# State space stage: three of the six exponentials of a batch stay in PSUM, and VectorE's work stands in another order

## The chip, the cores and the metric

One core of a Trainium2 chip runs the whole program. The metric is device time in microseconds, the median of the runs. Five engines run side by side, each in its own order, and meet only at semaphores: TensorE (PE, and PEld for its weight loads), VectorE (DVE), ScalarE (ACT), GpSimd (POOL), and the queue of SyncE (SP) that issues most DMAs.

## The reference, cut to what matters

The program is a decoder of two layers. The change is in the state space block, the first sublayer of the second layer, for 16 batches of 256 rows:

```
dt = softplus(dt + dt_bias);  A = -exp(A_log)
decay = exp(A * dt_t)
state = state * decay + (x_t * dt_t) * B_t        # for every t, 8 heads of 64, 128 states
y_t = einsum('bhpn,bn->bhp', state, C_t)
y = y + x_part * D_full
y = y * silu(z)
y = y * rsqrt(mean(y * y) + EPS) * norm_w
out = y @ out_proj_w.T
```

## The kernel before

`state_space` doesn't scan. It treats the 256 rows of a batch as two blocks of 128 and writes the scan as a product with a 128x128 matrix per head and block pair: exp(sum of A dt between the two rows) times the product of C and B. There are three block pairs (first with first, first with second, second with second) and 8 heads, so six tiles of 128x512 (four heads each), numbered u = 0 to 5; u // 2 is the block pair and u % 2 the half of the heads. For each u:

- `exponents(n, u)`, TensorE: two matmuls of 128x512 put the exponents of batch n into PSUM bank `e_ps[u % 2]`. So u = 0, 2, 4 share `e_ps[0]` and u = 1, 3, 5 share `e_ps[1]`. Before it writes u, it waits until the bank's last exponential was read (`decay_ready`).
- `decays(n, u)`, ScalarE: one exponential, from the bank into `mat[:, u]` in SBUF.
- `matrices(eng, n, u, ready)`: one multiplication of `mat[:, u]` by `gm`, the masked product of B and C, in place. VectorE does u = 0, 2, 4 (`low_mat_ready`), GpSimd u = 1, 3, 5 (`high_mat_ready`).
- `mix(n, blk)`, TensorE: multiplies the three finished tiles of one half of the heads by the scaled rows `xdt`.

Around them lie: `masked_products` (VectorE, makes `gm` from bank `g_ps`), `taps` (VectorE, three passes of the convolution over one projection bank `in_ps`, which frees that bank for the next `project`), `sum_experts` (VectorE, the input of batch n + 5: adds the experts' rows and takes their moments; then `scale_x` on GpSimd makes the norm's factors and ScalarE's `normalize_x` applies them), `tail_rows`, `high_terms` (VectorE, `rhs_hi` of the next batch's exponents; GpSimd's `low_terms` makes `rhs_lo`), `mean_squares`, `skip_terms`, `residual`, `gated`, `row_moments`, and `scaled_rows`, which makes `xdt` of the next batch from rows that `to_rows` has transposed into the two `e_ps` banks. `gather` on GpSimd issues the four indirect DMAs of batch n + 7.

The order on each engine is written out by hand in a loop over n (`STEPS`), with one branch for even and one for odd n, since the projections are done once for a pair of batches. In these loops two places matter for the argument. On ScalarE, in an even step, `decays(n, 1)` and `decays(n, 2)` stand behind `normalize_x(n + 4)`:

```
                    first_tap(n, 1)
                    if real(n + 4):
                        normalize_x(n + 4)
                    if now:
                        decays(n, 1)
                        decays(n, 2)
```

On GpSimd, in an odd step, `scale_x(n + 5)`, for which that `normalize_x` waits, stands behind `low_terms`, `scale_y` and `gather`, and the next even step begins with `split_y`'s products just done and u = 1 and 3 of `matrices`. `state_products(n)` on TensorE opens a batch; `project(n, i)` are six matmuls each, between the exponents.

## Time and profile before

| | us |
|---|---|
| median of 3 runs | 2675.45 (2670.41 to 2675.78) |
| the profiled execution | 2671.63 |
| its span | 2669.9 |
| the 16 batches of the state space stage | 1650 to 2030 of the span |

Outside that stretch the change touches no instruction that works on data. In the page the stage lies in slices 25 to 30 of 40. A busy engine there isn't yet a bound: the views further down show, in order of time, who waits for whom. In a timeline row the number in brackets is the idle time of the engine just before, and the arrow names what ended it; a row without brackets followed on the one ahead of it.

### The profile page before, as it was taken

What the parts mean: (1) busy time and instruction counts of PE and PEld (TensorE: products, weight loads), DVE (VectorE), ACT (ScalarE), POOL (GpSimd) and SP (SyncE); (2) the same over time, 40 slices, a digit from 0 to 9 for tenths busy, and PEclk for the clock granted to TensorE, in tenths of its full rate; (3) what the DMA queues carried; (4) which work ended last, traced back from release to release, by engine and by line L of the source; (5) the groups of instructions that cost most, each with busy time, mean ns of one, the idle gap of its engine ahead of it and who ended that gap; (6) DMA issues with size and microseconds to landing.
All of it is one profiled execution on the core that took longest, in us unless ns stands there. A gap on an engine that the chain in (4) does not pass through costs nothing. (4 is left out here: it accounts for less than half of the span.)

```text
span 2669.9 us, 63255 instructions
## 1 busy us (share of the span) xinstructions
PE 2341.5 (88%) x23480; PEld 1968.6 (74%) x23480; DVE 1950.1 (73%) x3223; ACT 1423.5 (53%) x2223; POOL 1619.4 (61%) x1937
## 2 busy tenths in 40 slices
PE   5999999997799877998999965988995899987998
PEld 4677777775566656998999964777774666756998
DVE  2677777776589872646888857999984588875776
ACT  2566666664466652335666544655652466653333
POOL 3667666764467751275666656777764587863443
PEclk9899999999899987999999987998996799988999
DMA  8566666551889841146666652111002887841111
GB/s 205 131 159 159 160 145 158 153 120 43 245 216 229 219 111 36 52 138 204 224 228 226 230 175 64 41 48 32 21 13 85 213 225 208 224 105 41 53 54 52
DMA packets 227288, 363.44 MB, mean 136 GB/s; under 512 B 51968, under 2 KB 156416, under 8 KB 219520
## 3 DMA queue, kind: packets, MB, share of 16 engines
q1 hardware_dynamic: 207392, 281.32, 39.7%
q0 software_dynamic: 17376, 78.13, 8.6%
q8 instruction: 143, 2.34, 0.4%
q10 hardware_dynamic: 2304, 1.05, 0.2%
q14 instruction: 73, 0.60, 0.1%
HBM read 231.72 MB, written 133.69 MB: 137 GB/s over the span
## 5 line engine op out<-in xcount | busy, mean ns | idle before, releaser
L1369 ACT ACTIVATE self_probs<-self_score_ps 128x768 f32<-128x768 f32 x256 | 208.7, 815 | 183.9 <-PE self_score_ps L1271 182.0
L1585 POOL TENSOR_SCALAR_AFFINE_SELECT self_probs<-self_probs 128x512 f32<-128x512 f32 x256 | 169.5, 663 | 158.6 <-ACT self_probs L1369 158.6
L1506 DVE TENSOR_REDUCE self_neg_max<-self_max_ps 128x2 f32<-128x256 f32 x256 | 108.1, 422 | 165.1 <-PE self_max_ps L88 165.1
L647 ACT ACTIVATE cross_probs<-cross_score_ps 128x1024 f32<-128x1024 f32 x128 | 131.2, 1025 | 101.6 <-PE cross_score_ps L545 100.0
L745 DVE TENSOR_REDUCE cross_neg_max<-cross_max_ps 128x4 f32<-128x1024 f32 x128 | 154.9, 1212 | 39.1 <-PE cross_max_ps L524 39.0
L1507 DVE TENSOR_REDUCE self_neg_max<-self_max_ps 128x2 f32<-128x512 f32 x256 | 174.5, 682 | 0.0
L2297 POOL TENSOR_TENSOR moee_h_lo<-moee_h,moee_h_hi 128x512 fp32r<-128x512 f32 x78 | 112.5, 1442 | 92.3 <-ACT moee_h_hi L2034 91.6
L739 DVE TENSOR_REDUCE causal_block_max<-causal_max_ps 128x6 f32<-128x768 f32 x128 | 120.9, 946 | 56.4 <-PE causal_max_ps L88 55.9
L3592 POOL TENSOR_TENSOR ffn_g_lo<-ffn_g_full,ffn_g_hi 128x512 fp32r<-128x512 f32 x64 | 82.1, 1283 | 129.2 <-ACT ffn_g_hi L3478 116.9
L2034 ACT ACTIVATE moee_h_hi<-moee_h 128x512 fp32r<-128x512 f32 x110 | 69.6, 632 | 163.2 <-DVE moee_h L2200 163.2
L647 ACT ACTIVATE causal_probs<-causal_score_ps 128x768 f32<-128x768 f32 x128 | 103.6, 809 | 99.2 <-PE causal_score_ps L545 99.0
L79 PE MATMUL moee_g_ps<-moee_x_hi,moee_in_hi 128*128 128x256 f32 x440 | 131.3, 298 | 10.0 <-DVE moee_x_lo L2187 5.8
L1271 PE MATMUL self_score_ps<-self_q_stack,self_k_stack 49*128 49x128 f32 (+1 forms) x1024 | 129.0, 330 | 10.0 <-ACT self_probs L1369 6.4
L2200 DVE TENSOR_TENSOR moee_h<-moee_u_ps,moee_silu 128x512 f32<-128x512 f32 x110 | 75.5, 686 | 82.0 <-PE moee_u_ps L81 77.4
L2240 POOL DMA_INDIRECT x_tiles<-kept_x,moek_slot x64 | 65.8, 1029 | 107.1 <-issue 104.1
L79 PE MATMUL moee_y_ps<-moee_out_hi,moee_h_hi 128*128 128x256 f32 x440 | 125.4, 285 | 0.7 <-DVE moee_out_lo L2152 0.7
L81 PE MATMUL moee_g_ps<-moee_x_hi,moee_in_lo 128*128 128x256 f32 x440 | 125.7, 286 | 0.0
L79 PE MATMUL moee_u_ps<-moee_x_hi,moee_in_hi 128*128 128x256 f32 x440 | 125.7, 286 | 0.0
L80 PE MATMUL moee_g_ps<-moee_x_lo,moee_in_hi 128*128 128x256 f32 x440 | 125.7, 286 | 0.0
L80 PE MATMUL moee_u_ps<-moee_x_lo,moee_in_hi 128*128 128x256 f32 x440 | 125.1, 284 | 0.0
L81 PE MATMUL moee_u_ps<-moee_x_hi,moee_in_lo 128*128 128x256 f32 x440 | 125.1, 284 | 0.0
L81 PE MATMUL moee_y_ps<-moee_out_hi,moee_h_lo 128*128 128x256 f32 x440 | 124.9, 284 | 0.0
(507 smaller groups left out, 9479.9 us busy)
## 6 DMA issues: line engine op xcount, KB each, us to landing
self_q<-self_q_split SPq DMA_DIRECT2D x48, 512.0 KB, 3.5
self_q_raw<-self_q SPq DMA_DIRECT2D x32, 768.0 KB, 8.2
cross_stacks<-cross_qk SPq DMA_DIRECT2D x64, 384.0 KB, 6.4
causal_stacks<-causal_qk SPq DMA_DIRECT2D x64, 384.0 KB, 6.4
moe_y_tiles<-lasting_y_out SPq DMA_DIRECT2D x55, 256.0 KB, 2.5
mid<-lasting_y_out SPq DMA_DIRECT2D x48, 256.0 KB, 2.2
x_tiles<-zeros SPq DMA_DIRECT2D x16, 624.0 KB, 5.5
moee_xT<-x_tiles SPq DMA_DIRECT2D x39, 256.0 KB, 7.3
```

The costliest lines, as they stand in the source:

```text
L79: pe.matmul(out, a[0], b[0], start=start, stop=False, **kw)
L80: pe.matmul(out, a[0], b[1], start=False, stop=False, **kw)
L81: return pe.matmul(out, a[1], b[0], start=False, stop=stop, **kw)
L647: nc.scalar.activation(probs[i // 2][:, a, :, lo:], score_ps[:, :, lo:], ACT.Exp, scale=HD ** -0.5).then_inc(prob_ready, 1)
L739: last = dve.tensor_reduce(block_max[:, :, col % 4, :], bank[:, :, 0:3 * P].rearrange("p a (j t) -> p a j t", t=P), AX.X, ALU.max, negate= ...
L745: last = dve.tensor_reduce(neg_max[p][:, tile, :, col % 4, :], bank[:].rearrange("p a (q k) -> p a q k", q=QT), AX.X, ALU.max, negate=True)
L1271: last = pe.matmul(score_ps[:, ab, j * S + k * P:(j + 1) * S], k_stack[p][rows, tile, k * P:(k + 1) * P], q_stack[rows, 4 * tile + c, k * P:],
L1369: nc.scalar.activation(probs[g % 4][:, a, :, P:], score_ps[:, :, P:], ACT.Exp, scale=HD ** -0.5).then_inc(prob_ready, 1)
L1506: dve.tensor_reduce(neg_max[:, tile, :, c, 0:1], bank[:, :, 0:P], AX.X, ALU.max, negate=True)
L1507: dve.tensor_reduce(neg_max[:, tile, :, c, 1:2], bank[:, :, S:2 * S], AX.X, ALU.max, negate=True).then_inc(max_kept, 1)
L1585: pool.affine_select(diagonal, diagonal, [[0, 2], [0, 2], [1, P]], ALU.is_ge, zero, base=0, channel_multiplier=-1).then_inc(prob_masked, 1)
L2297: pool.tensor_tensor(h_lo[p][f][:].rearrange("p j s -> p (j s)"), h[f][:], h_hi[p][f][:].bitcast(F32).rearrange("p j s -> p (j s)"), ALU.s ...
```

## The change

Three things, all in the state space stage:

1. `decays(n, u)` for even u writes its exponential back into `e_ps[0]` in place of `mat`. `matrices` on VectorE reads it from there and writes `mat`; so one of its inputs lies in PSUM. Odd u is as before, on GpSimd.
2. The bank is now free only once VectorE has multiplied. `exponents(n, 2)` and `exponents(n, 4)` wait for `low_mat_ready` of u = 0 and u = 2, and `to_rows(n + 1)` of that bank waits for that of u = 4. The wait for `ssm_done` (that `mat` is free) moves from u = 0 on ScalarE to u = 1, and for u = 0 to VectorE.
3. VectorE's order is changed, so that the multiplications come sooner.

```diff
                 if u in (0, 2):
                     pe.wait_ge(rhi_ready, 2 * n + 1 + u // 2)
                     pe.wait_ge(rlo_ready, 2 * n + 1 + u // 2)
-                if u >= 2:
+                if u in (2, 4):
+                    pe.wait_ge(low_mat_ready, 3 * n + u // 2)
+                elif u >= 2:
                     pe.wait_ge(decay_ready, 6 * n + u - 1)
...
-                    if b:
-                        pe.wait_ge(decay_ready, 6 * b - 1 + q)
+                    if b and q == 0:
+                        pe.wait_ge(low_mat_ready, 3 * b)
+                    elif b:
+                        pe.wait_ge(decay_ready, 6 * b)
...
                 act.wait_ge(e_done, 6 * n + u + 1)
-                if u == 0 and n:
+                if u == 1 and n:
                     act.wait_ge(ssm_done, 2 * n)
-                nc.scalar.activation(mat[:, u, :, :].rearrange("p h t -> p (h t)"), e_ps[u % 2][:],
-                                     ACT.Exp).then_inc(decay_ready, 1)
+                dst = mat[:, u, :, :].rearrange("p h t -> p (h t)") if u % 2 else e_ps[0][:]
+                nc.scalar.activation(dst, e_ps[u % 2][:], ACT.Exp).then_inc(decay_ready, 1)
...
-            eng.tensor_tensor(mat[:, u, :, :], mat[:, u, :, :],
+            src = mat[:, u, :, :] if u % 2 else e_ps[0][:].rearrange("p (h t) -> p h t", t=P)
+            if u == 0 and n:
+                eng.wait_ge(ssm_done, 2 * n)
+            eng.tensor_tensor(mat[:, u, :, :], src,
```

VectorE, even batch (batch 4; the names are those of the section on the kernel). Before, `sum_experts` comes first (its last row here), then `gm`, `taps` 0 and 1 (three rows each), the multiplications of u = 0 and 2 together, `tail_rows`, `high_terms` and u = 4:

```order
L2859 BN_AGGR ssm_c_mv<-ssm_c_stats 128x2 x2
L2939 TENSOR_TENSOR ssm_gm<-ssm_g_ps,ssm_triang 128x384
L2893 SCALAR_TENSOR_TENSOR ssm_bc<-ssm_in_ps,ssm_cw,ssm_bc 128x2x255
L2893 SCALAR_TENSOR_TENSOR ssm_bc<-ssm_in_ps,ssm_cw,ssm_bc 128x2x254
L2893 SCALAR_TENSOR_TENSOR ssm_bc<-ssm_in_ps,ssm_cw,ssm_bc 128x2x253
L2893 SCALAR_TENSOR_TENSOR ssm_bc<-ssm_in_ps,ssm_cw,ssm_bc 128x2x255
L2893 SCALAR_TENSOR_TENSOR ssm_bc<-ssm_in_ps,ssm_cw,ssm_bc 128x2x254
L2893 SCALAR_TENSOR_TENSOR ssm_bc<-ssm_in_ps,ssm_cw,ssm_bc 128x2x253
L2827 TENSOR_TENSOR ssm_mat<-ssm_mat,ssm_gm 128x512 x2
L2947 TENSOR_TENSOR ssm_xdt_tail<-ssm_xdt,ssm_tail 128x512
L2930 TENSOR_TENSOR ssm_rhs_hi<-ssm_triang,ssm_a_hi 128x1024 x2
L2827 TENSOR_TENSOR ssm_mat<-ssm_mat,ssm_gm 128x512
```

Now the batch begins with `gm`; u = 0 stands ahead of `taps` 0, u = 2 between the two `taps`, and `sum_experts` behind them:

```order
L2946 TENSOR_TENSOR ssm_gm<-ssm_g_ps,ssm_triang 128x384
L2834 TENSOR_TENSOR ssm_mat<-ssm_e_ps,ssm_gm 128x512
L2900 SCALAR_TENSOR_TENSOR ssm_bc<-ssm_in_ps,ssm_cw,ssm_bc 128x2x255
L2900 SCALAR_TENSOR_TENSOR ssm_bc<-ssm_in_ps,ssm_cw,ssm_bc 128x2x254
L2900 SCALAR_TENSOR_TENSOR ssm_bc<-ssm_in_ps,ssm_cw,ssm_bc 128x2x253
L2834 TENSOR_TENSOR ssm_mat<-ssm_e_ps,ssm_gm 128x512
L2900 SCALAR_TENSOR_TENSOR ssm_bc<-ssm_in_ps,ssm_cw,ssm_bc 128x2x255
L2900 SCALAR_TENSOR_TENSOR ssm_bc<-ssm_in_ps,ssm_cw,ssm_bc 128x2x254
L2900 SCALAR_TENSOR_TENSOR ssm_bc<-ssm_in_ps,ssm_cw,ssm_bc 128x2x253
L2874 SCALAR_TENSOR_TENSOR ssm_y_shared<-ssm_y_routed,moek_weight,ssm_y_shared 128x256 x2
L2881 SCALAR_TENSOR_TENSOR ssm_x<-ssm_y_routed,moek_weight,ssm_y_shared 128x256 x2
L2862 BN_STATS ssm_c_stats<-ssm_x 128x6 x2
```

The same batch, some rows further on: `tail_rows`, then u = 4, which has moved ahead of `high_terms`, and `taps` 2:

```order
L2866 BN_AGGR ssm_c_mv<-ssm_c_stats 128x2 x2
L2954 TENSOR_TENSOR ssm_xdt_tail<-ssm_xdt,ssm_tail 128x512
L2834 TENSOR_TENSOR ssm_mat<-ssm_e_ps,ssm_gm 128x512
L2937 TENSOR_TENSOR ssm_rhs_hi<-ssm_triang,ssm_a_hi 128x1024 x2
L2900 SCALAR_TENSOR_TENSOR ssm_xs<-ssm_in_ps,ssm_cw,ssm_xs 128x2x255
L2900 SCALAR_TENSOR_TENSOR ssm_xs<-ssm_in_ps,ssm_cw,ssm_xs 128x2x254
L2900 SCALAR_TENSOR_TENSOR ssm_xs<-ssm_in_ps,ssm_cw,ssm_xs 128x2x253
```

What moved there: all three multiplications come earlier among VectorE's rows, and `sum_experts` and `high_terms` later.

VectorE, odd batch (batch 5). Before, u = 0 and 2 stand together behind `sum_experts`; u = 4 is the row after the last one here, behind `ms`:

```order
L2939 TENSOR_TENSOR ssm_gm<-ssm_g_ps,ssm_triang 128x384
L2867 SCALAR_TENSOR_TENSOR ssm_y_shared<-ssm_y_routed,moek_weight,ssm_y_shared 128x256 x2
L2874 SCALAR_TENSOR_TENSOR ssm_x<-ssm_y_routed,moek_weight,ssm_y_shared 128x256 x2
L2855 BN_STATS ssm_c_stats<-ssm_x 128x6 x2
L2857 MEMSET ssm_gate 128x1
L2859 BN_AGGR ssm_c_mv<-ssm_c_stats 128x2 x2
L2827 TENSOR_TENSOR ssm_mat<-ssm_mat,ssm_gm 128x512 x2
L2947 TENSOR_TENSOR ssm_xdt_tail<-ssm_xdt,ssm_tail 128x512
L2893 SCALAR_TENSOR_TENSOR ssm_xs<-ssm_in_ps,ssm_cw,ssm_xs 128x2x255
L2893 SCALAR_TENSOR_TENSOR ssm_xs<-ssm_in_ps,ssm_cw,ssm_xs 128x2x254
L2893 SCALAR_TENSOR_TENSOR ssm_xs<-ssm_in_ps,ssm_cw,ssm_xs 128x2x253
L2962 TENSOR_SCALAR ssm_ms<-ssm_g_ps 128x2
```

Now u = 0 stands ahead of `sum_experts` and u = 2 still behind it; u = 4 is the row after the last one here, ahead of `ms`:

```order
L2946 TENSOR_TENSOR ssm_gm<-ssm_g_ps,ssm_triang 128x384
L2834 TENSOR_TENSOR ssm_mat<-ssm_e_ps,ssm_gm 128x512
L2874 SCALAR_TENSOR_TENSOR ssm_y_shared<-ssm_y_routed,moek_weight,ssm_y_shared 128x256 x2
L2881 SCALAR_TENSOR_TENSOR ssm_x<-ssm_y_routed,moek_weight,ssm_y_shared 128x256 x2
L2862 BN_STATS ssm_c_stats<-ssm_x 128x6 x2
L2864 MEMSET ssm_gate 128x1
L2866 BN_AGGR ssm_c_mv<-ssm_c_stats 128x2 x2
L2834 TENSOR_TENSOR ssm_mat<-ssm_e_ps,ssm_gm 128x512
L2954 TENSOR_TENSOR ssm_xdt_tail<-ssm_xdt,ssm_tail 128x512
L2900 SCALAR_TENSOR_TENSOR ssm_xs<-ssm_in_ps,ssm_cw,ssm_xs 128x2x255
L2900 SCALAR_TENSOR_TENSOR ssm_xs<-ssm_in_ps,ssm_cw,ssm_xs 128x2x254
L2900 SCALAR_TENSOR_TENSOR ssm_xs<-ssm_in_ps,ssm_cw,ssm_xs 128x2x253
```

What moved there is u = 0, ahead of the eight rows or so of `sum_experts`, and `ms` behind u = 4. On the other engines no instruction that works on data moves.

## Rows read from the trace of the kernel before

**Rows 1.** Busy time by window: stretch, length, busy (instructions) by engine, clock, DMA.

```profile
1746.70:1796.70 50.00, 43.78 (x307) 37.09 (x307) 47.99 (x89) 30.24 (x50) 38.42 (x40) 0.97 0.15 43
```

**Rows 2.** Tiles ssm_mat and ssm_e_ps, instructions: min/median/max ns, first and last start.

```profile
L2827 DVE TENSOR_TENSOR ssm_mat<-ssm_mat,ssm_gm x48: 656/790/2387, 1658.3 to 2021.6; 128x512 f32<-128x512 f32 x48
...
L2955 DVE TENSOR_TENSOR ssm_xdt<-ssm_e_ps,ssm_dt x32: 656/681/691, 1646.1 to 2011.7; 128x512 f32<-128x512 f32 x32
```

**Rows 3.** Groups by line and shape, VectorE, 1650 to 2030 us.

```profile
L2827 DVE TENSOR_TENSOR ssm_mat<-ssm_mat,ssm_gm 128x512 f32<-128x512 f32 x48 | 52.3, 1110 | 6.4 <-ACT ssm_mat L2670 6.1
...
L2947 DVE TENSOR_TENSOR ssm_xdt_tail<-ssm_xdt,ssm_tail 128x512 f32<-128x512 f32 x16 | 18.5, 1157 | 0.0
```

**Rows 4.** Timeline, VectorE, batch 4: start, length, instruction [idle before <- releaser].

```profile
1743.74 3.01 DVE L2930 TENSOR_TENSOR ssm_rhs_hi<-ssm_triang,ssm_a_hi 128x1024 fp32r<-128x1024 f32 x2
1746.68 0.87 DVE L2867 SCALAR_TENSOR_TENSOR ssm_y_shared<-ssm_y_routed,moek_weight,ssm_y_shared 128x256 f32<-128x256 f32 x2
...
1749.45 0.52 DVE L2939 TENSOR_TENSOR ssm_gm<-ssm_g_ps,ssm_triang 128x384 f32<-128x384 f32 x1
1749.89 4.52 DVE L2893 SCALAR_TENSOR_TENSOR ssm_bc<-ssm_in_ps,ssm_cw,ssm_bc 128x510 f32<-128x510 f32 x6
1754.32 2.59 DVE L2827 TENSOR_TENSOR ssm_mat<-ssm_mat,ssm_gm 128x512 f32<-128x512 f32 x2
1756.84 1.77 DVE L2947 TENSOR_TENSOR ssm_xdt_tail<-ssm_xdt,ssm_tail 128x512 f32<-128x512 f32 x1
1758.53 2.35 DVE L2930 TENSOR_TENSOR ssm_rhs_hi<-ssm_triang,ssm_a_hi 128x1024 fp32r<-128x1024 f32 x2
1760.80 0.68 DVE L2827 TENSOR_TENSOR ssm_mat<-ssm_mat,ssm_gm 128x512 f32<-128x512 f32 x1
...
1766.34 0.87 DVE L2990 SCALAR_TENSOR_TENSOR ssm_yz<-ssm_xs,ssm_dcol,ssm_y_ps 128x256 f32<-128x256 f32 x2 [0.36 <-PE ssm_y_ps L2554]
...
1770.91 1.26 DVE L2955 TENSOR_TENSOR ssm_xdt<-ssm_e_ps,ssm_dt 128x512 f32<-128x512 f32 x2
```

**Rows 5.** Timeline, ScalarE, batch 4.

```profile
1748.71 0.60 ACT L2670 ACTIVATE ssm_mat<-ssm_e_ps 128x512 f32<-128x512 f32 x1
...
1752.25 1.09 ACT L2731 ACTIVATE ssm_x<-ssm_x,ssm_c_shift,ssm_c_rstd 128x256 f32<-128x256 f32 x2 [1.73 <-POOL ssm_c_shift L3102]
1753.25 1.06 ACT L2670 ACTIVATE ssm_mat<-ssm_e_ps 128x512 f32<-128x512 f32 x2
```

**Rows 6.** Timeline, GpSimd, batches 4 to 6.

```profile
1752.03 0.18 POOL L3102 TENSOR_TENSOR ssm_c_shift<-ssm_c_low,ssm_c_rstd 128x2 f32<-128x2 f32 x1
...
1771.14 0.23 POOL L3097 TENSOR_SCALAR ssm_var<-ssm_mv 128x2 f32<-128x2 f32 x1 [2.89 <-issue]
...
1788.46 1.90 POOL L3127 TENSOR_TENSOR ssm_rhs_lo<-ssm_triang,ssm_a_lo 128x1024 fp32r<-128x1024 f32 x1 [0.90 <-DVE ssm_a_lo L2924]
...
1802.04 0.18 POOL L3102 TENSOR_TENSOR ssm_c_shift<-ssm_c_low,ssm_c_rstd 128x2 f32<-128x2 f32 x1
```

**Rows 7.** Timeline, TensorE, batches 4 and 5.

```profile
1753.87 0.50 PE L2526 MATMUL ssm_e_ps<-ssm_rhs_hi,ssm_one_r 128*128 128x512 f32 x1 [3.72 <-ACT ssm_mat L2670]
...
1778.53 0.40 PE L2526 MATMUL ssm_e_ps<-ssm_rhs_hi,ssm_after 128*128 128x512 f32 x1
...
1785.87 0.40 PE L2552 MATMUL ssm_y_ps<-ssm_mat,ssm_xdt_tail 128*64 128x128 f32 x2 [1.63 <-DVE ssm_mat L2827]
```

**Rows 8.** Timeline, VectorE, batch 5, and the end of batch 6.

```profile
1775.46 1.91 DVE L2867 SCALAR_TENSOR_TENSOR ssm_y_shared<-ssm_y_routed,moek_weight,ssm_y_shared 128x256 f32<-128x256 f32 x2
...
1779.28 1.26 DVE L2827 TENSOR_TENSOR ssm_mat<-ssm_mat,ssm_gm 128x512 f32<-128x512 f32 x2
...
1783.35 2.37 DVE L2827 TENSOR_TENSOR ssm_mat<-ssm_mat,ssm_gm 128x512 f32<-128x512 f32 x1
1786.40 0.88 DVE L2971 SCALAR_TENSOR_TENSOR lasting_y_out<-ssm_xT_ps,ssm_row_scale,ssm_x 128x256 f32<-128x256 f32 x2 [0.68 <-issue]
...
1822.04 1.25 DVE L2955 TENSOR_TENSOR ssm_xdt<-ssm_e_ps,ssm_dt 128x512 f32<-128x512 f32 x2
```

More of the change, by code:

```diff
@@ L3010, in _ @@
                 if n % 2 == 0:
+                    if now:
+                        masked_products(n)
+                        matrices(dve, n, 0, low_mat_ready)
+                    taps(n, 0)
+                    if now:
+                        matrices(dve, n, 2, low_mat_ready)
+                    taps(n, 1)
                     if real(n + 5) and n != -2:
@@ L3013, in _ @@
                     if now:
-                        masked_products(n)
-                    taps(n, 0)
-                    taps(n, 1)
+                        tail_rows(n)
                     if now:
-                        matrices(dve, n, 0, low_mat_ready)
-                        matrices(dve, n, 2, low_mat_ready)
-                        tail_rows(n)
+                        matrices(dve, n, 4, low_mat_ready)
                     if n >= 0 and soon:
                         high_terms(n + 1)
-                    if now:
-                        matrices(dve, n, 4, low_mat_ready)
                     taps(n, 2)
@@ L3050, in _ @@
                         masked_products(n)
+                        matrices(dve, n, 0, low_mat_ready)
                     if real(n + 5):
@@ L3053, in _ @@
                     if now:
-                        matrices(dve, n, 0, low_mat_ready)
                         matrices(dve, n, 2, low_mat_ready)
@@ L3057, in _ @@
                     taps(n, 0)
+                    if now:
+                        matrices(dve, n, 4, low_mat_ready)
                     if late:
                         mean_squares(n - 1)
-                    if now:
-                        matrices(dve, n, 4, low_mat_ready)
                     if late:
```

## The prediction

> **What bounds the kernel now.** I read the windows first. In one period of two batches, 50.00 us long, VectorE is busy 47.99 us and TensorE 43.78 [rows 1]. So VectorE has 2 us of slack in 50, and the stage looks bound by it. The second look is at the length of its multiplications: at line L2827 they take from 656 to 2387 ns for one and the same shape [rows 2], 1110 ns in the mean, and `tail_rows` 1157 ns [rows 3]. A product that reads PSUM in one input (`scaled_rows`, same shape) takes 656 to 691 ns all 32 times [rows 2]. The long ones lie where GpSimd multiplies too. That is what the change goes for: 48 x (1110 - 680) = 20.6 us of stretching in `mat`, and 16 x (1157 - 680) = 7.6 us in `tail_rows`, beside it.
>
> The third look, at the timelines, is the one that decides. The even batch has a chain that doesn't run through VectorE's busy time. GpSimd ends `c_shift` of `scale_x` at 1752.03 [rows 6]; only then do ScalarE's `normalize_x` (1752.25, after 1.73 us of waiting) and, behind it, the exponentials of u = 1 and 2 run, which end at 1753.25 + 1.06 = 1754.31 [rows 5]. TensorE waits 3.72 us for them [rows 7]. VectorE doesn't wait: it spends this time on `sum_experts` and both `taps`, and comes to the multiplications at 1754.32, when u = 2 has just been done [rows 4]. So before, VectorE's order covers a late GpSimd exactly. I call R the end of `row_moments`, where `scaled_rows` starts (1770.91 for batch 4 [rows 4], 1822.04 for batch 6 [rows 8]). From R to the next `c_shift` are 1802.04 - 1770.91 = 31.13 us [rows 6]. There GpSimd goes through `scale_y` (1771.14), `scale_x`, `split_y`, `gather`, its products, the row scale, a short turn to VectorE for `residual` and `a_lo` (GpSimd idles 0.90 us for it at 1788.46), `low_terms` and the next `gather`. From `c_shift` to R are 1770.91 - 1752.03 = 18.88 us in batch 4 and 20.00 in batch 6. The sum of the two is the period.
>
> **The change, part by part.**
>
> *Multiplying from PSUM.* 48 instructions on VectorE lose their stretching. In a pair like 4 and 5: u = 0 and 2 of the even batch take 2.59 us for two [rows 4] where two unstretched ones take 1.26 [rows 8], so 1.33 less; `tail_rows` 1.77, or 0.68 once it no longer falls beside GpSimd's products, 1.09 less [rows 4]; u = 4 of the odd batch 2.37 [rows 8] against 0.68, 1.69 less. That is 4.1 us of VectorE's time in a pair. The ScalarE side is the same instruction with another target; no row shows a write back into its bank. I bound it by 0 to 0.6 us (the whole instruction, [rows 5]) for each of 48, and take 0, since it has idle time around it.
>
> The Trainium skill, "VectorE: DVE Perf Modes", section on the TRN2 errata, gives an instruction from PSUM 120 fixed cycles and one from SBUF 58; at its 0.96 GHz that would be an estimated 0.065 us more for each, 3.1 us for 48. The trace has the two alike, 681 ns and 680 or so for the unstretched ones, and the sum leaves it out.
>
> *VectorE's new order in the even batch.* After `rhs_hi`, at 1746.68 [rows 4], VectorE now needs `gm` at once. Before, `gm` came at 1749.45, with nothing to wait for; now it waits for TensorE's products of B and C, which I put at about 1747.4, 0.7 us. Then u = 0 needs the first exponential, 1748.71 + 0.60 = 1749.31 [rows 5]: 1.4 us more. It is followed by `taps` 0 (4.43 us for six rows [rows 4], so 2.22), to 1752.2; and u = 2 needs 1754.31: 2.1 us of waiting. Together 4.2 us of idle time, where there was none. What is queued behind it: `taps` 1, `sum_experts`, `tail_rows`, u = 4, `high_terms`, `taps` 2 and 3. From `c_shift` on the sum is: to the end of the second exponential 2.28 and to VectorE 0.05; u = 2 0.60; `taps` 1 2.22; `sum_experts` 1749.45 - 1746.68 = 2.77; `tail_rows` 0.60; u = 4 0.60; `high_terms` 1760.80 - 1758.53 = 2.27; `taps` 2 and 3 with `mean_squares` 4.51; and from `skip_terms` to R 1770.91 - 1766.34 = 4.57. That makes 20.47 us against 18.88 before, **1.6 us more**. In the other direction, `high_terms` now begins when GpSimd begins u = 5; where it collides it takes 1746.68 - 1743.74 = 2.94, and the loss is 2.3 us. In batch 6 the same stretch took 20.00 us with the same work on VectorE, so part of it was waiting, which the longer new order covers; against it the loss is 0.5 to 1.1 us. So VectorE's saving of 2.4 us in the even batch is less than the 4.2 us it now waits.
>
> *TensorE's waits.* `exponents(n, 2)` waits for the product u = 0, at 1750.0 instead of 1749.5; it was idle for 3.72 us right behind it [rows 7], so this costs nothing. In the odd batch `exponents(n, 4)` waits for u = 2, which still stands behind `sum_experts`. It stood at 1778.53, R + 7.62 [rows 7]. u = 2 now ends at about R + 9.6: `gm` and u = 0 to R + 5.15, `sum_experts` with its stretched first rows 1779.28 - 1775.46 = 3.82 [rows 8], u = 2 0.60. So TensorE's `output`, behind it, moves by 2.0 us. It had 1.63 us in hand, the wait of `mix` for u = 4 [rows 7], so `mix` starts 0.4 us later; `residual`, which stood at R + 15.49 waiting for the row scale [rows 8], now waits for `output` until R + 15.4. The 1.69 us that u = 4 gives back are therefore spent waiting. The odd batch saves nothing, and 31.13 us stay 31.13.
>
> *The moved wait for `ssm_done`* costs nothing: `mix` of the batch before is over some 8 us before u = 0 or 1 is due.
>
> **The sum.** A pair then takes 51.6 to 52.3 us, where 4 and 5 took 50 and the one up to batch 6's R 51.13. I count batches 2 and 4 with 1.6 to 2.3 us, 6 and 8 with 0.5 to 1.1, 0 and 10 with about 2 each (there `c_shift` is early, but VectorE still waits for the first exponential and for u = 2), 1 us for the odd batch 1, where nothing on GpSimd is late, and nothing for batches 11 to 15: there VectorE is no longer full, a saving finds no taker, and the longer hand-over from TensorE over ScalarE and VectorE back costs as much as it gives. That is 9 to 12 us; I take 9.5. Against the profiled execution, 2671.63, that is 2681. That execution lies at the fast end of the runs, whose median is 2675.45; I set the time between the two sums, at **2683**.
>
> **The rivals.**
>
> *A, faster: the stretching was the bound and the new waits go away.* If `c_shift` came 2 us earlier, or VectorE came later to u = 2, the 28 us of stretching would come out in full: 2647, or with half of it hidden by TensorE's 43.78 us in 50, some 2662. For it speak rows 1 and 3: VectorE has the least slack, and 28 us is much. Against it: `c_shift` waits for GpSimd, whose list isn't shortened. It decides from the point where GpSimd's 31.13 us fall below about 29.5. The rule behind A is the Trainium skill's, "SBUF — State Buffer", section "Who interferes with whom": a VectorE instruction with one SBUF input doesn't contend with GpSimd, one with two does; the rows agree with it. Chance 18%.
>
> *B, no change: both cancel.* The waits come as I say, but half of `sum_experts`' stretching (1.05 us, 3.82 against 2.77) and of the gather's goes too, since neither meets a product of VectorE that reads SBUF twice, and GpSimd's part shrinks by 1 to 1.5 us in a pair. Eight pairs then give -5 to +5 us: 2671 to 2680. Chance 24%.
>
> *C, slower by more: the odd batch becomes a bound too.* If `exponents(n, 4)` waits longer than TensorE's 1.63 us in hand by 2 us more, or reading PSUM doesn't end the stretching after all (1.33 + 1.69 us a pair come back), each pair loses another 2 to 3 us, in all 16 to 26 more: 2692 to 2702. Against the second speak the 32 products of `scaled_rows`, none stretched. Chance 6%.
>
> **How the numbers follow.** My forecast (5 to 16 us slower) has 52%, C 6%, B 24%, A 18%. About 0.2%, 5.3 us, is what a measurement of this kernel can tell from no change. So slower 0.58, same 0.24, faster 0.18. The range leaves out C and the larger part of A: from 2665 to 2692.
>
> **What would show it.** Right: the multiplications of VectorE all take 0.65 to 0.7 us; rows of u = 0 and of u = 2 in the even batches have idle time ahead of them that the exponential ends, some 1.4 and 2 us; `c_shift` still comes about 31 us after R; TensorE waits for a VectorE `mat` before `exponents(n, 4)` in odd batches; VectorE's busy time in the stage falls by some 25 us and its idle time grows by more. Wrong: periods under 50 us, or multiplications over 0.7 us. What would make the prediction wrong is above all GpSimd's part: if with VectorE's reads gone its products, `split_y` and `gather` run through quicker than I count, `c_shift` comes earlier and every period with it.

## The result

The changed kernel takes **2692.08 us** (median of 7 runs, 2683.45 to 2694.15); the kernel before, beside it, 2673.28 us (7 runs, 2670.41 to 2675.78). The ratio is **1.0064**, with a 95% interval of 1.0049 to 1.0079: slower, by 13 to 21 us. The forecast was 2683 in a range of 2665 to 2692. The direction held, and so did the mechanism of the even batches. The size didn't: the forecast had 7.5 us over its 2675.45 us, less than half of the 18.8 us between the two medians, and the time lies at the very end of a wide range.

The profiled execution of the changed kernel took 2692.08 us, with a span of 2690.3. First the answer to [rows 1], for a stretch as long as the new period:

```profile
1755.50:1807.40 51.90, 44.39 (x307) 36.54 (x307) 44.58 (x88) 30.54 (x49) 37.09 (x41) 0.97 0.14 41
```

VectorE has lost 3.4 us of work in a pair of batches (47.99 to 44.58), and the pair takes 1.9 us more than the 50.00 of [rows 1]. The work went where it was to go. The tile view (min/median/max ns) and the groups by line, of after, answer to [rows 2] and [rows 3]:

```profile
L2834 DVE TENSOR_TENSOR ssm_mat<-ssm_e_ps,ssm_gm x48: 656/690/693, 1657.6 to 2036.9; 128x512 f32<-128x512 f32 x48
...
L2834 POOL TENSOR_TENSOR ssm_mat<-ssm_mat,ssm_gm x48: 1265/1284/2232, 1660.4 to 2043.8; 128x512 f32<-128x512 f32 x48
```

```profile
L2834 DVE TENSOR_TENSOR ssm_mat<-ssm_e_ps,ssm_gm 128x512 f32<-128x512 f32 x48 | 32.9, 685 | 30.3 <-ACT ssm_e_ps L2675 29.7
L2954 DVE TENSOR_TENSOR ssm_xdt_tail<-ssm_xdt,ssm_tail 128x512 f32<-128x512 f32 x16 | 14.1, 878 | 0.0
```

None of the 48 multiplications takes more than 693 ns, where the longest took 2387. Their group has fallen from 52.3 us to 32.9, but the idle time just ahead of them (the first number behind the second bar) has risen from 6.4 us to 30.3. That pair of numbers is the core of the result: 19.4 us of work went, and 23.9 us of waiting came.

VectorE in batch 4 of after, against [rows 4] and [rows 8], with the next pair's end as the last row:

```profile
1754.27 3.00 DVE L2937 TENSOR_TENSOR ssm_rhs_hi<-ssm_triang,ssm_a_hi 128x1024 fp32r<-128x1024 f32 x2
1758.04 0.56 DVE L2946 TENSOR_TENSOR ssm_gm<-ssm_g_ps,ssm_triang 128x384 f32<-128x384 f32 x1 [0.76 <-PE ssm_g_ps L2513]
1759.94 0.69 DVE L2834 TENSOR_TENSOR ssm_mat<-ssm_e_ps,ssm_gm 128x512 f32<-128x512 f32 x1 [1.35 <-ACT ssm_e_ps L2675]
1760.55 2.30 DVE L2900 SCALAR_TENSOR_TENSOR ssm_bc<-ssm_in_ps,ssm_cw,ssm_bc 128x510 f32<-128x510 f32 x3
1764.67 0.69 DVE L2834 TENSOR_TENSOR ssm_mat<-ssm_e_ps,ssm_gm 128x512 f32<-128x512 f32 x1 [1.81 <-ACT ssm_e_ps L2675]
...
1771.45 3.44 DVE L2937 TENSOR_TENSOR ssm_rhs_hi<-ssm_triang,ssm_a_hi 128x1024 fp32r<-128x1024 f32 x2
...
1783.86 1.25 DVE L2962 TENSOR_TENSOR ssm_xdt<-ssm_e_ps,ssm_dt 128x512 f32<-128x512 f32 x2
...
1835.79 1.25 DVE L2962 TENSOR_TENSOR ssm_xdt<-ssm_e_ps,ssm_dt 128x512 f32<-128x512 f32 x2
```

The three waits of the forecast are there, 0.76, 1.35 and 1.81 us, in all 3.9 where 4.2 were put down. One row shows what the forecast had not: `high_terms` (`rhs_hi`) at 1771.45 takes 3.44 us. Over the stage that group has grown from 46.3 us to 53.9, so VectorE lost part of its saving again. ScalarE and GpSimd, against [rows 5] and [rows 6], show what the third stands on:

```profile
1762.58 1.09 ACT L2735 ACTIVATE ssm_x<-ssm_x,ssm_c_shift,ssm_c_rstd 128x256 f32<-128x256 f32 x2 [1.43 <-POOL ssm_c_shift L3110]
1763.58 0.57 ACT L2675 ACTIVATE ssm_mat<-ssm_e_ps 128x512 f32<-128x512 f32 x1
1764.05 0.58 ACT L2675 ACTIVATE ssm_e_ps<-ssm_e_ps 128x512 f32<-128x512 f32 x1
```

```profile
1762.36 0.18 POOL L3110 TENSOR_TENSOR ssm_c_shift<-ssm_c_low,ssm_c_rstd 128x2 f32<-128x2 f32 x1
...
1814.29 0.18 POOL L3110 TENSOR_TENSOR ssm_c_shift<-ssm_c_low,ssm_c_rstd 128x2 f32<-128x2 f32 x1
```

From `c_shift` to R are 21.50 us (before: 18.88), from R to the next `c_shift` 30.43 (before: 31.13). The second exponential, now one into its own bank, still stands behind `normalize_x`, and that behind `c_shift`. In the odd batch 5 VectorE waits twice, and the rest stands as it stood:

```profile
1797.48 0.16 DVE L2969 TENSOR_SCALAR ssm_ms<-ssm_g_ps 128x2 f32<-128x2 f32 x1 [0.97 <-PE ssm_g_ps L2579]
1799.00 0.88 DVE L2978 SCALAR_TENSOR_TENSOR lasting_y_out<-ssm_xT_ps,ssm_row_scale,ssm_x 128x256 f32<-128x256 f32 x2 [1.36 <-PE ssm_xT_ps L81]
```

All the kernels that follow are read by the same marks: S is the first `scaled_rows` (batch 0), R0 to R14 those at the end of the even batches, and "last" is the start of the last `residual` (R10 to R12, 45.0 to 48.1 us in all but the two with the odd order, is left out). All times in the table are us, from the profiled execution of each; the ratio to the kernel before has its 95% interval, and the median of the kernel before, in the runs beside each, lay between 2673 and 2684 us, which is why ratios and not times are set side by side.

| kernel | S to R0 | R0 to R2 | pairs R2 to R10 | R12 to R14 | R14 to last | S to last | ratio |
|---|---|---|---|---|---|---|---|
| before | 26.85 | 47.88 | 50.04, 51.13, 51.38, 48.19 | 43.94 | 29.75 | 394.7 | |
| before again | 26.18 | 47.87 | 50.02, 51.22, 51.40, 48.19 | 43.96 | 29.77 | 394.2 | |
| after | 30.36 | 52.64 | 51.87, 51.93, 52.18, 50.39 | 43.48 | 35.34 | 414.5 | 1.0064 (1.0049 to 1.0079) |
| order alone | 32.05 | 53.44 | 53.07, 53.13, 53.45, 51.44 | 40.46 | 33.84 | 416.1 | 1.0063 (1.0040 to 1.0087) |
| bank alone | 27.01 | 55.23 | 56.00, 54.86, 56.44, 55.99 | 43.48 | 35.34 | 432.5 | 1.0150 (1.0117 to 1.0184) |
| sum first | 23.90 | 51.44 | 49.32, 49.54, 49.57, 47.15 | 46.66 | 35.38 | 398.0 | 1.0027 (1.0008 to 1.0047) |
| exponentials first | 28.38 | 51.27 | 50.47, 50.57, 50.84, 49.45 | 46.70 | 35.61 | 408.4 | 1.0066 (1.0029 to 1.0102) |
| both moves | 23.46 | 48.20 | 47.37, 47.44, 47.71, 47.16 | 46.69 | 35.58 | 388.7 | 0.9969 (0.9955 to 0.9983) |
| before, exponentials first | 27.10 | 48.57 | 50.76, 50.76, 51.09, 48.29 | 46.60 | 29.75 | 398.5 | 1.0014 (0.9997 to 1.0031) |
| last two in SBUF | 30.24 | 52.66 | 51.87, 51.91, 51.12, 50.39 | 41.00 | 34.07 | 409.6 | 1.0050 (1.0029 to 1.0070) |
| filled end | 28.84 | 52.67 | 51.88, 50.84, 51.13, 49.80 | 45.78 | 30.10 | 406.1 | 1.0038 (1.0023 to 1.0052) |
| both moves, odd order | 25.82 | 56.13 | 55.69, 54.34, 53.76, 60.02 | 54.43 | 35.23 | 448.8 | 1.0183 (1.0149 to 1.0217) |
| the same, end mended | 25.80 | 56.11 | 55.69, 53.48, 56.03, 58.79 | 47.45 | 24.73 | 431.4 | 1.0140 (1.0109 to 1.0170) |
| both moves, end mended | 25.01 | 48.21 | 47.38, 47.44, 47.73, 47.12 | 40.73 | 24.72 | 373.4 | 0.9924 (0.9909 to 0.9940) |

### The profile page after: what moved, and what is told of

The parts are those of the page before. It is cut to its first block and busy times, and to the rows that moved or that the text cites. A ratio compares the mean times of both kernels' runs of the same rounds, so it can differ in the third digit from the quotient of the medians.

```text
span 2690.3 us, 63255 instructions
## 1 busy us (share of the span) xinstructions
PE 2350.3 (87%) x23480; PEld 1970.1 (73%) x23480; DVE 1930.6 (72%) x3223; ACT 1425.1 (53%) x2223; POOL 1608.9 (60%) x1937
## 5 line engine op out<-in xcount | busy, mean ns | idle before, releaser
L80 PE MATMUL moee_y_ps<-moee_out_lo,moee_h_hi 128*128 128x256 f32 x440 | 124.9, 284 | 0.0
```

The lines of the kernel that those rows point to most:

```text
L80: pe.matmul(out, a[0], b[1], start=False, stop=False, **kw)
```

## The experiments

### What is not the kernel's doing

> The kernel before once more, for its trace. It tells what of the differences is not the kernel's doing. From the first batch's lower_x to the last residual it took 395.3 us in its first trace, the changed kernel 415.1; I expect 395 within 1 us again, pairs of 50 to 51.4 us, and a stage that begins up to 10 us later or earlier than at 1645.5. Open: the output of batch 14 ran in 4.2 us in the first trace and takes 7.9 us (TensorE at half its clock) in the traces of the changed kernel and of all its variants. If the 4.2 us was chance, it takes 7.9 here and the stage 399; if it belongs to the kernel, 4.2.

Every pair came out within 0.1 us of the first trace, and the whole stage within 0.6. S, though, stood at 1649.81 against 1646.14: the stages ahead of this one vary by some us from run to run. The 2.85 us by which S stood later in the changed kernel (1648.99) are therefore no finding. The output of batch 14, TensorE's last product of a batch (`ssm_xT_ps`), took 4.3 us again, so that belongs to the kernel and is no chance. Here and below an output's length goes from the start of its first product to the start of its last group of three: 4.26 us in the first trace and here. A window over all of it is some 0.5 us longer.

### The two parts apart

Order alone has VectorE's new order, and of the placement this is taken back, with the waits that go with it:

```diff
-                dst = mat[:, u, :, :].rearrange("p h t -> p (h t)") if u % 2 else e_ps[0][:]
+                dst = mat[:, u, :, :].rearrange("p h t -> p (h t)")
```

> VectorE's new order alone; all six exponentials go to SBUF as in the kernel before. Theory (the lost time comes from the order: in even batches VectorE reaches its products before ScalarE has the exponentials, and sum_experts, which covered that, now stands behind c_shift; the time lost at the end of the stage comes from the bank's hand-over): the pairs from batch 2 to 10 take 51 to 52 us as in the changed kernel, TensorE no longer waits for products before exponents, and the 5.6 us after batch 14's row_moments go; 2684 to 2690 against 2692 of the changed kernel's profiled execution. Rival (the bank is what costs): the pairs fall back to 50 to 51 us and the time to that of the kernel before, 2668 to 2676. Second rival (stretched products come back on top): products over 1 us in the mean and pairs of 53 us or more, 2695 or more.

The pairs took 53.1 us, beyond the 51 to 52 of the theory, and the median of 2695.98 us is beyond its 2684 to 2690. By its marks the second rival held: pairs of 53 or more, products over 1 us in the mean, 2695 or more. Against the kernel before, the whole came to what the changed kernel takes. So in this order the bank saves about 1.2 us in a pair (53.13 against 51.93), and the order costs 2.0 to 3.3 against the kernel before. The products' mean here:

```profile
L2828 DVE TENSOR_TENSOR ssm_mat<-ssm_mat,ssm_gm 128x512 f32<-128x512 f32 x48 | 50.4, 1051 | 25.7 <-ACT ssm_mat L2671 24.9
```

They are still stretched, and they wait 24.9 us for ScalarE without the bank: most of the 29.7 us of waiting in the changed kernel is the order's. The part of the expectation on the end of the stage fell. Only 1.5 of the 5.6 us behind R14 went, with the bank's hand-over gone. The windows of order alone, ahead of the output of batch 14 and over it, tell why (the column behind the engines is the granted clock of TensorE):

```profile
2042.80:2047.00 4.20, 4.12 (x10) 2.85 (x11) 3.59 (x3) 2.41 (x6) 3.79 (x3) 0.50 0.21 68
2047.00:2055.00 8.00, 8.00 (x40) 8.00 (x38) 1.27 (x3) 0.47 (x1) 1.93 (x2) 0.50 0.00 0
```

TensorE is busy all the time and is granted 0.50, the lower of its two levels (1.2 instead of 2.4 GHz). The same output in the kernel before, and in the changed kernel:

```profile
2018.20:2022.90 4.70, 4.70 (x41) 4.55 (x39) 1.89 (x3) 0.81 (x2) 1.72 (x3) 1.00 0.02 3
```

```profile
2036.90:2045.40 8.50, 8.50 (x41) 8.43 (x39) 0.84 (x2) 0.60 (x1) 1.93 (x2) 0.50 0.00 0
```

It is the same 41 records of matrix products, in 4.7 us and in 8.5. So a second cause is at work behind R14, the clock.

Bank alone is the other half: the exponentials in their bank, and VectorE's whole order as before, which begins, in the even batches:

```diff
                 if n % 2 == 0:
-                    if now:
-                        masked_products(n)
-                        matrices(dve, n, 0, low_mat_ready)
-                    taps(n, 0)
-                    if now:
-                        matrices(dve, n, 2, low_mat_ready)
-                    taps(n, 1)
                     if real(n + 5) and n != -2:
                         sum_experts(n + 5)
                     if now:
+                        masked_products(n)
+                    taps(n, 0)
+                    taps(n, 1)
+                    if now:
+                        matrices(dve, n, 0, low_mat_ready)
+                        matrices(dve, n, 2, low_mat_ready)
                         tail_rows(n)
...
```

> The exponentials of u = 0, 2 and 4 in their bank alone; VectorE's order as in the kernel before. Theory: exponents for u = 2 now wait for the product of u = 0, which stands behind sum_experts and both taps; the second exponential and the product of u = 2 follow some 3 us later, so the even batches lose more than the 2.4 us that unstretched products save: pairs of 51 to 53 us, 2684 to 2700, with the time at the end of the stage lost as in the changed kernel. Rival (order is all that costs, the bank is free or gives its saving): pairs below 50 us, 2650 to 2668.

Worse than the theory had it: pairs of 54.9 to 56.4 us instead of 51 to 53, and a median of 2715.54 us. TensorE in the even batch 4:

```profile
1776.82 0.77 PE L2528 MATMUL ssm_e_ps<-ssm_rhs_hi,ssm_one_r 128*128 128x512 f32 x1 [5.35 <-DVE ssm_mat L2834]
```

It waits 5.35 us for the first product, which stands behind `sum_experts` and both taps, and the exponents come at half the clock behind that wait (0.77 for the first, where it takes 0.47 to 0.50 at full). In the order of before the bank costs more than it gives, 3.7 to 7.8 us a pair; it needs another order, and the one that came with it costs too.

### The two waits that the order opened

Sum first, against the changed kernel:

```diff
                 if n % 2 == 0:
+                    if real(n + 5) and n != -2:
+                        sum_experts(n + 5)
                     if now:
                         masked_products(n)
                         matrices(dve, n, 0, low_mat_ready)
...
-                    if real(n + 5) and n != -2:
-                        sum_experts(n + 5)
```

> The changed kernel with sum_experts back at the front of the even batches on VectorE, ahead of masked_products. Theory: it fills the 0.8 us of waiting for the products of B and C and the 1.35 us for the first exponential, and no longer stands between c_shift and row_moments; the stretch from c_shift to row_moments falls from 20.5 to about 18.5 us, the pairs of batches 2 to 10 from 51.9 to 49.5 to 50.2 us, in all 9 to 14 us less than the changed kernel: 2677 to 2682 on the scale of 2691. Rival 1 (GpSimd's side moves with it, since sum_experts then falls beside its products): no change, within 4 us. Rival 2 (the unstretched products were a gain that the order hid, and it comes out in full): pairs of 48 us or less, 2665 or less.

Pairs of 49.3 to 49.6 us, 2.4 to 2.6 less, as the theory had it or a little better. The stage is 16.5 us shorter, though R12 to R14 took 3.2 us more, with the output of batch 13 at 7.9 us. The waits for `gm` and for the first exponential are gone, the one for the second stays:

```profile
1763.42 0.69 DVE L2834 TENSOR_TENSOR ssm_mat<-ssm_e_ps,ssm_gm 128x512 f32<-128x512 f32 x1
1764.03 2.30 DVE L2900 SCALAR_TENSOR_TENSOR ssm_bc<-ssm_in_ps,ssm_cw,ssm_bc 128x510 f32<-128x510 f32 x3
1767.69 0.69 DVE L2834 TENSOR_TENSOR ssm_mat<-ssm_e_ps,ssm_gm 128x512 f32<-128x512 f32 x1 [1.36 <-ACT ssm_e_ps L2675]
```

Exponentials first, against the changed kernel, is an edit on ScalarE in the even batches:

```diff
+                    if now:
+                        decays(n, 1)
+                        decays(n, 2)
                     if real(n + 4):
                         normalize_x(n + 4)
                     if now:
-                        decays(n, 1)
-                        decays(n, 2)
                         tails(n)
```

> The changed kernel with ScalarE's exponentials of u = 1 and 2 ahead of normalize_x in the even batches, so that they no longer wait for GpSimd's c_shift. Theory: VectorE's wait of 1.8 us for the second exponential goes, taps and sum_experts come forward by as much and the path from c_shift to row_moments is VectorE's own work; the pairs of batches 2 to 10 fall from 51.9 to 48.5 to 50.5 us, in all 7 to 17 us less: 2675 to 2684 on the scale of 2691. Rival 1 (what c_shift really releases is something else, tails or the sum's data, so nothing moves): within 3 us. Rival 2 (normalize_x one exponential later delays TensorE's transposes and with them the next batch): 3 us or more slower.

The mirror image: the wait for the second exponential is gone, the first two stay (0.76 and 1.35 us at 1756.84 and 1758.75), and the first three pairs fall by 1.3 to 1.4 us, to 50.5 to 50.8, just past the upper end of the theory. R12 to R14 took 3.2 us more than in the changed kernel (46.70 against 43.48): the output of batch 13 now took 7.9 us, of which more below. In the times, whose interval is wide here, the gain of 6 us in the stage doesn't show.

> The changed kernel with both moves: sum_experts back at the front of the even batches on VectorE, and ScalarE's exponentials of u = 1 and 2 ahead of normalize_x. With the first alone the even batch took 28.2 us and still held 1.36 us of waiting for the second exponential and 0.90 for the third; with the second alone 29.4. Theory: VectorE then waits for nothing in the even batch, which takes 26.0 to 26.8 us, a pair 47.1 to 48; from batch 2 to 10 that is 15 to 20 us less than the changed kernel, and the unstretched products pay at last: 2672 to 2680 on the scale of 2691, a ratio to the kernel before of 0.993 to 0.999. Rival 1: GpSimd's list becomes the bound, and the pair stays at 49 us or more. Rival 2: what the pairs gain is lost to TensorE at half its clock in the batches 12 to 15, which now come with more idle time: pairs of 47 to 48 us, but 24 us or more from batch 12's row_moments to batch 14's.

With both edits pairs take 47.4 us, 4.5 less than in the changed kernel and more than the sum of the two alone (2.5 and 1.4). The granted clock over the pair below is 1.00, where it was 0.97 in the pairs shown of both kernels (0.93 in the next pair of the kernel before), so a part of the gain may be the clock's:

```profile
1751.70:1799.10 47.40, 42.72 (x308) 35.41 (x307) 43.92 (x88) 30.30 (x48) 37.68 (x41) 1.00 0.15 45
```

This one is faster than the kernel before: 0.9969 (0.9955 to 0.9983). The first rival fell, and the second holds: R12 to R14 takes 46.69 us and R14 to last 35.58, 8.6 us more than before. The change pays, once VectorE has something else to do until the exponential is there, and the exponential doesn't stand behind `c_shift`. How much of that is the bank's is not shown: no run has both moves with all exponentials in SBUF.

> The kernel before, with ScalarE's exponentials of u = 1 and 2 ahead of normalize_x in the even batches; nothing else. TensorE's wait of 3.7 us goes. Theory: the pairs here are VectorE's own stretched work (48 us busy in 50) and c_shift of the next pair, so the move gives little: pairs of 49 to 51 us, 0 to 5 us less than the kernel before. Rival (the hand-over behind c_shift bounds the kernel before too): pairs of 48 us or less, 10 to 20 us less.

It has ScalarE's edit of above and nothing else of the change. Nothing was gained: pairs of 50.8 to 51.1 us, a ratio of 1.0014 (0.9997 to 1.0031). So TensorE's 3.72 us of [rows 7] were not what bounded the kernel before, whose VectorE was busy for 48 of 50 us. R12 to R14 grew by 2.7 us here, by the output of batch 13 (7.89 us against 5.13). The 6 us of stage that both moves gain over the kernel before therefore need more than ScalarE's edit: the bank, VectorE's new order, or both.

### The end of the stage

Last two in SBUF, against the changed kernel, with the waits to match:

```diff
-                dst = mat[:, u, :, :].rearrange("p h t -> p (h t)") if u % 2 else e_ps[0][:]
+                dst = mat[:, u, :, :].rearrange("p h t -> p (h t)") if u % 2 or n >= 14 else e_ps[0][:]
```

> The changed kernel, but in batches 14 and 15, where VectorE has little to do, the exponentials of u = 0, 2 and 4 go to SBUF and the waits are those of the kernel before. Theory: of the 5.6 us that the changed kernel loses after batch 14's row_moments, 1.5 are the longer hand-over (TensorE, ScalarE, VectorE and back) and 4.1 are the output of batch 14 at half of TensorE's clock. The hand-over goes in both batches: row_moments of 12 to those of 14 take 40.5 to 42.5 us against 43.5, and 33.8 us from there to the last residual against 35.3; 3 to 5 us off the whole, and the output of batch 14 still takes 7.9 us. Rival (the whole 5.6 us is the hand-over): 30 us from row_moments to the last residual.

R12 to R14 fell by 2.5 us and R14 to last by 1.3, as the theory had it, and the output of batch 14 stayed at 7.9. In the ratio (1.0050 against 1.0064) the intervals overlap, so this rests on the traces.

Filled end, against the changed kernel, calls the function below on TensorE, 6 ahead of exponents 2 in batch 14, 6 ahead of exponents 0 and of 2 in batch 15, and 13 ahead of the output of batch 15. All that the reference computes is still computed.

```diff
+            def fill(count):
+                free_bank(88)
+                free_bank(89)
+                for _ in range(count):
+                    pe.matmul(in_ps[0][:], w_hi[:, 0, 0:P], x_hi[1][:, 0, :], start=True, stop=True)
```

> The changed kernel with matrix products of no use (512 columns, into a bank of the input projections that nobody reads any more) in TensorE's waits of the last batches: 6 ahead of exponents for u = 2 in batches 14 and 15, 6 ahead of u = 0 in batch 15, 13 ahead of the output of batch 15. Theory: output of batches 14 and 15 takes 7.9 us each in the changed kernel because TensorE's clock is granted at half after its waits; with the waits filled it takes 4.3 us each time, and from batch 14's row_moments to the last residual are 28 to 31 us against 35.3: 4 to 7 us off the whole. Rival (the clock doesn't depend on these waits): 7.9 us again and the fill costs up to 1.5 us.

R14 to last fell by 5.2 us to 30.10. The windows over the outputs of batches 13, 14 and 15:

```profile
2011.60:2019.50 7.90, 7.90 (x39) 7.90 (x38) 4.20 (x4) 0.60 (x1) 3.85 (x4) 0.50 0.00 0
2034.40:2038.70 4.30, 4.30 (x38) 4.25 (x38) 1.40 (x3) 0.86 (x2) 0.81 (x3) 1.00 0.00 0
2048.30:2056.20 7.90, 7.90 (x37) 7.90 (x38) 0.16 (x1) 0.00 (x0) 0.69 (x1) 0.50 0.00 0
```

Batch 14 is at full clock again, so the clock was the larger part of the lost end. It was more than the output's length. The start of batch 14's output, in us behind R14, with the exponentials of that batch in SBUF or in the bank, and the output at either clock:

| exponentials | output at 1.00 | output at 0.50 |
|---|---|---|
| in SBUF | 7.12 (before) | 7.32 (order alone, last two in SBUF) |
| in the bank | 7.45 (filled end) | 8.76 (after) |

With the clock kept, the bank's longer hand-over costs 0.3 us; together with the low clock it costs 1.6. On the other hand batch 13, partly spared in the changed kernel (5.3 us), ran at half here, and R12 to R14 took 2.3 us more. Kernels without the fill show the same (sum first, exponentials first, both moves, and before with exponentials first), so whether the fill did it is not shown. TensorE waited 2.71 us between the 13 products and batch 15's output, which ran at half as in the kernel before: for that output the rival held.

### A step too far, and the best kernel

Both moves, odd order, changes VectorE's odd batch against both moves:

```diff
                         matrices(dve, n, 0, low_mat_ready)
-                    if real(n + 5):
-                        sum_experts(n + 5)
+                    taps(n, 0)
                     if now:
                         matrices(dve, n, 2, low_mat_ready)
                         tail_rows(n)
-                    taps(n, 0)
+                    if real(n + 5):
+                        sum_experts(n + 5)
```

> The kernel with both moves, and in the odd batches VectorE does the tap of unit 0 between the products of u = 0 and 2, and sum_experts only behind tail_rows. With both moves alone the odd batch took 21.1 us, of which VectorE waits 0.97 us for the sum of squares and 1.36 for the output, since exponents for u = 4 wait for the product of u = 2 behind sum_experts. Theory: that wait of TensorE's comes 0.5 to 2 us earlier, and the odd batch takes 19 to 20.5 us, a pair 45.5 to 47 against 47.4: 3 to 8 us off. Rival 1: VectorE now waits for the second exponential instead, because the tap is shorter than sum_experts (2.3 against 2.8 us), and nothing moves, within 2 us. Rival 2: sum_experts falls beside GpSimd's gather and its products, and GpSimd's list, 26 us an even batch, gets longer by what VectorE saves.

A clear miss: pairs of 54 to 60 us instead of 45.5 to 47. VectorE and TensorE in an odd batch:

```profile
1795.92 2.31 DVE L2901 SCALAR_TENSOR_TENSOR ssm_xs<-ssm_in_ps,ssm_cw,ssm_xs 128x510 f32<-128x510 f32 x3 [3.06 <-ACT ssm_xs L2693]
1798.15 0.68 DVE L2835 TENSOR_TENSOR ssm_mat<-ssm_e_ps,ssm_gm 128x512 f32<-128x512 f32 x1
1798.75 2.83 DVE L2955 TENSOR_TENSOR ssm_xdt_tail<-ssm_xdt,ssm_tail 128x512 f32<-128x512 f32 x1
```

```profile
1798.88 0.50 PE L2528 MATMUL ssm_e_ps<-ssm_rhs_hi,ssm_after 128*128 128x512 f32 x1 [3.30 <-DVE ssm_mat L2835]
```

It is the mistake of the change once more, and I had the rows to see it: the tap's first step is ScalarE's, and that came at 1795.12, 2.3 us after VectorE was free. `sum_experts` had covered it. The product of u = 2 starts 6.0 us behind that of u = 0 (1792.17), where it stood 3.85 behind in the changed kernel with `sum_experts` between them, and TensorE waits 3.30 us for it. `tail_rows`, which reads SBUF twice, is stretched to 2.83 us on top. And behind TensorE's wait the clock falls. This is the window over the output that follows, the output of batch 4:

```profile
1800.10:1808.00 7.90, 7.90 (x40) 7.75 (x39) 4.88 (x12) 6.48 (x8) 2.90 (x3) 0.53 0.00 1
```

The outputs of batches 0, 2, 4, 6, 8 and 10, which run in the odd steps, took 7.1 to 7.9 us here, and 4.26 each with both moves. That is 2.9 to 3.6 us of the 6.0 to 12.9 that a pair lost. Neither rival had the late tap or the clock.

> All that has helped, together: both moves, the odd batch's other order, the last two batches' exponentials in SBUF, and products of no use in TensorE's waits at the end (6 ahead of u = 2 in batches 14 and 15, 9 ahead of u = 0 in batch 15, 23 ahead of the output of batch 15). Theory: the pairs as with both moves or 1 to 2 us less, and 27 to 31 us from batch 14's row_moments to the last residual against 35.6, with the output of batch 14 at 4.3 us: 8 to 16 us less than with both moves alone, 2660 to 2668 and a ratio to the kernel before of 0.991 to 0.995. Rival (the clock's fall is put off and not undone, as the fill did in the batch before): 4 us or less.

The pairs inherit that miss, and the whole took 2714.30 us where 2660 to 2668 were expected. The end didn't: R14 to last took 24.73 us. So the last kernel is both moves, the last two batches in SBUF and the larger fill, with the odd batch left as it was.

> The kernel with both moves, and its end mended: the last two batches' exponentials in SBUF, and products of no use in TensorE's waits (6 ahead of u = 2 in batches 14 and 15, 9 ahead of u = 0 in batch 15, 23 ahead of the output of batch 15); the odd batches keep the changed kernel's order, since the other order made VectorE wait 3.06 us for the first tap of unit 0. Theory: pairs as with both moves (47.4 us), the output of batches 13, 14 and 15 at 4.3 us each, 39 to 43 us from batch 12's row_moments to batch 14's (46.7 with both moves alone) and 24 to 26 from there to the last residual (35.6): 13 to 18 us less than with both moves alone, a ratio to the kernel before of 0.990 to 0.994. Rival (the fill merely shifts where the clock falls, since it also did so in batch 13): 5 us or less, a ratio of 0.995 or more.

All of the theory held. The ratio is **0.9924 (0.9909 to 0.9940)**, 16 to 24 us faster than the kernel before, and this is the best of all. The windows over the outputs of batches 13, 14 and 15:

```profile
1988.10:1992.80 4.70, 4.70 (x42) 4.57 (x40) 4.70 (x4) 0.74 (x2) 2.77 (x2) 1.00 0.00 0
2006.20:2011.00 4.80, 4.80 (x42) 4.64 (x41) 2.98 (x4) 0.82 (x2) 2.91 (x3) 1.00 0.00 0
2020.00:2024.90 4.90, 4.85 (x40) 4.67 (x40) 0.16 (x1) 0.00 (x0) 0.69 (x1) 1.00 0.00 0
```

Against both moves alone, R12 to last is 65.45 us instead of 82.27. No run has the fill without the placement, or the placement without the fill, on top of both moves, so how the 16.8 us divide between them is not shown. Nor has any run the fill on the kernel before, whose outputs of batches 13 and 15 are slow too (5.1 and 8.0 us against 4.26 and 4.34 here): of the 16 to 24 us, what the fill brings might be had without the change.

## Why the prediction was right, and where it was too small

By its own steps, with the changed kernel's numbers:

- *What bounds the kernel.* Right for the changed kernel: VectorE's busy time fell by 19.2 us over the stage (350.84 to 331.68, S to the last row), and the stage became 19.8 us longer (394.7 to 414.5). For the kernel before it is right in part only. The prediction let the chain over `c_shift` decide there; taken off that chain, the kernel before gained nothing (1.0014), so VectorE's own work bounded it at least as much.
- *VectorE's busy time falls by some 25 us.* It was 19.2. The multiplications and `tail_rows` gave 23.9, and `high_terms`, which reads SBUF twice, took 7.6 back (46.3 to 53.9). The sum had allowed for its collision in the even batches, with 0.67 us each.
- *Writing back into the bank costs ScalarE nothing.* Right: 582 ns in the median for 48 exponentials into their bank, 592 for 48 into SBUF.
- *The stretching of `mat` goes.* Right: 19.4 us of 20.6. That of `tail_rows` went in part only: 1157 ns to 878, 4.5 us of 7.6. It still has two inputs in SBUF. In the even batches it moved away from GpSimd's products; in batch 1 it took 2.86 us.
- *The waits of the even batch.* Right: 0.76, 1.35 and 1.81 us against 0.7, 1.4 and 2.1.
- *From `c_shift` to R.* 21.50 us against 20.47 to 21.14. The difference is `high_terms`, which meets GpSimd's product and takes 3.44 us where the sum had 2.27, and 2.94 for a collision.
- *The odd batch saves nothing.* Right: exponents for u = 4 start at R + 9.29 (forecast R + 9.6) behind 1.16 us of waiting, and `residual` at R + 15.14 (R + 15.4), released by the output.
- *The pairs.* 51.87, 51.93 and 52.18 from R2 to R8, against 51.6 to 52.3. Batches 4, 6, 8 and 10 came to 1.8, 0.8, 0.8 and 2.2 us; forecast were 1.6 to 2.3, 0.5 to 1.1 twice, and about 2.
- *The start* was too small. S to R0 grew by 3.5 us, forecast 2: with `sum_experts` gone from the front, `gm` of batch 0 waits 3.27 us, where the forecast had named only the exponentials' waits, and `high_terms` takes 4.53 us there, where it took 2.35 before. R0 to R2 grew by 4.8, forecast 2.6 to 3.3. Batch 1's part of that is 2.3, not 1, by the 2.86 us of `tail_rows` above.
- *"Nothing for batches 11 to 15"* is **the step that failed**: it was 5.9 us. R14 to last grew from 29.75 to 35.34. The prediction said that the longer hand-over there costs as much as the saving gives. The output of batch 14 starts 8.8 us behind R14 instead of 7.1, and it then runs at half the clock, 7.9 us instead of 4.3. The two aren't independent: filled end, which keeps the hand-over and restores the clock, took away 5.2 us of the 5.6 behind R14, and last two in SBUF, which does the reverse, 1.3. So the hand-over alone was put nearly right (0.3 us too low), and what failed is that the clock of TensorE had no term.

The terms that stood in the sum gave 9 to 12 us. Put in as measured they give: start 3.5, batches 1 and 2 4.8, batches 3 to 10 5.6, the rest 5.9, together 19.8. Of the 10 us that were missing, 5.9 are the end, and most of that the clock. That the time still fell at the range's end is owed to the range, which had been made wide for the rivals and not for this. Rival A had its condition right, the hand-over behind `c_shift` and not VectorE's work, and both moves show its price: 6 us of stage against the kernel before, not 28, before the end is mended. As for the rule of the Trainium skill behind it ("SBUF — State Buffer", section "Who interferes with whom"), the trace agrees: with one input in PSUM none of 48 is over 693 ns. From PSUM the multiplications take 685 ns in the mean, and the 24 unstretched ones of the kernel before, with both inputs in SBUF, 679. The Trainium skill's other rule cited ("VectorE: DVE Perf Modes", section on the TRN2 errata), from which the prediction estimated 65 ns more for each, doesn't show in them; the measurement decides.

## What to carry over

An instruction order that looks idle-free is often covering something: ask of each piece of work moved away from the front of a late operand what it was hiding, and read the operand's arrival from the row of its producer, first step included (behind the tap's late ScalarE step VectorE waited 3.06 us and TensorE 3.30, and the clock fell). A saving on the busiest engine is worth little while the next operand comes at a fixed time behind another engine; move the producer first, then take the saving (both moves: 0.9969, where the change had 1.0064). In a stage's last batches, where nothing overlaps, count hand-overs in full and look at the granted clock.

## What the runs showed that I had not expected

The clock of TensorE takes part in the result. An output at the lower level takes 7.9 us instead of 4.3. In six kernels (after, bank alone, sum first, exponentials first, both moves, odd order) TensorE waited 2.6 us ahead of exponents for u = 2 of batch 14, and the clock was at 0.50 behind that wait; the output of batch 13, next in line, took 5.3 us in the first two and 7.9 in the rest. The length of the wait doesn't decide it alone: it was 1.85 us in the kernel before and 1.87 in the same with exponentials first, and the output took 5.1 us in one and 7.9 in the other. The kernel before and order alone have nearly the same waits behind R14 (2.29 and 1.53 us against 2.33 and 1.52), and yet the clock was back for the output in one and not in the other: it was low from 3.5 to 6.9 us behind R14 in the kernel before, and from 2.1 to 15.7 in order alone, where TensorE was busy for the last 12 us of it. What sets its return stays open; that both traces of the kernel before show the same says that it isn't mere chance. In the best kernel, with matrix products of no use in the waits and the last two batches in SBUF, the clock stayed at 1.00 through the outputs of batches 13, 14 and 15.
